# Moving half a unit of row norms, two head sums and a semaphore count inside a fused four-block network

## The reference

```
pQ, pK = elu(Q), elu(K)                       # 16 heads of 16
kv = einsum('bshe,bshd->bsed', K, V) * SCALE  # per row, over the heads
attn = w1 - lmb * w2                          # w = einsum(Q, kv), per row
attn = (1 - LAMBDA_INIT) * rms(attn, g2)      # head norm: over 16 numbers
attn = rms(attn, g3) + attn                   # row norm: over 256 numbers
h = gelu(attn @ W1.T);  out = h @ W2.T + attn
x = layernorm(x + out)
```

## Time and profile before

| | |
|---|---|
| median of 3 runs | 947.38 us (947.28 to 952.99) |
| profiled execution, its own time | 946.61 us |
| span of the profile | 945.0 us |
| mean granted clock of TensorE | 0.951 of full |
| busy PE / PEld / DVE / ACT / POOL | 831.6 / 688.2 / 616.9 / 482.5 / 254.4 us |

### The profile page before, as it was taken

One profiled execution on the slowest core, in us unless ns is written; L12 is line 12 of the kernel. 1 busy time (PEld: TensorE's weight loads), 2 busy tenths in 40 slices (PEclk: granted clock), 3 DMA queues, 4 the chain that ended last, 5 costly groups with the idle time before them and its releaser, 6 DMA issues. The chain is left out here.

```text
span 945.0 us, 23205 instructions
## 1 busy us (share of the span) xinstructions
PE 831.6 (88%) x8838; PEld 688.2 (73%) x8838; DVE 616.9 (65%) x1408; ACT 482.5 (51%) x999; POOL 254.4 (27%) x323
## 2 busy tenths in 40 slices
PE   5999999999799999998999889889888949999960
PEld 5777787877577777766677778776666738999960
DVE  2577777777557777777565435678666885666626
ACT  2544434434567777766964334554644232635425
POOL 1256655121112222223000000013232121656444
PEclk9999999999999999999999999999988858999995
DMA  8500000000000000002466344443222301657429
GB/s 320 168 18 17 22 17 17 17 17 2 1 1 1 1 1 1 1 1 68 130 184 187 94 116 114 119 125 132 90 91 73 106 20 40 200 136 213 120 40 345
DMA packets 76429, 79.56 MB, mean 84 GB/s; under 512 B 22592, under 2 KB 66496, under 8 KB 75968
## 3 DMA queue, kind: packets, MB, share of 16 engines
q1 hardware_dynamic: 71376, 72.36, 24.8%
q0 software_dynamic: 3968, 5.25, 3.2%
q10 hardware_dynamic: 1008, 0.91, 0.3%
HBM read 50.71 MB, written 27.79 MB: 83 GB/s over the span
## 5 line engine op out<-in xcount | busy, mean ns | idle before, releaser
L713 DVE TENSOR_TENSOR r_prob<-r_pS,const 128x512 f32<-128x512 f32 x128 | 79.4, 681 | 32.4 <-PE r_pS L540 32.4
L1087 DVE SCALAR_TENSOR_TENSOR f_gl<-att_res,small_first,f_gh 128x512 fp32r<-128x512 f32 x64 | 47.3, 747 | 37.3 <-ACT f_gh L1012 35.0
L941 PE MATMUL f_pY<-wpjT,f_gh 128*128 128x256 f32 x256 | 66.1, 292 | 0.3 <-DVE f_gl L1087 0.3
L942 PE MATMUL f_pY<-wpjT,f_gl 128*128 128x256 f32 x256 | 63.4, 281 | 0.0
L1347 PEld LDWEIGHTS q_bank<-q_xT,att_res 128*64 128x64 f32 x1024 | 55.6, 137 | 7.2 <-issue 4.2
L941 PEld LDWEIGHTS f_pY<-wpjT,f_gh 128*128 128x128 f32 x256 | 48.7, 190 | 15.9 <-issue 13.4
L2418 POOL DMA_INDIRECT sum_dram<-e_yo,y_id x24 | 43.1, 1796 | 63.5 <-ACT e_yo L2551 47.7
L1347 PE MATMUL q_bank<-q_xT,att_res 128*64 128x128 f32 x1024 | 59.2, 274 | 0.0
L1006 ACT ACTIVATE att_res<-f_pH 128x512 f32<-128x512 f32 x64 | 38.1, 595 | 40.1 <-PE f_pH L926 39.4
L2532 ACT ACTIVATE e_hh<-e_pH 128x320 fp32r<-128x320 f32 x64 | 26.2, 434 | 55.7 <-PE e_pH L2457 55.5
L837 POOL TENSOR_SCALAR t_ey<-t_es 128x8 f32<-128x8 f32 x4 | 0.8, 203 | 197.3 <-ACT t_sqrow L1908 197.3
(11 more groups left out here) (307 smaller groups left out, 2368.5 us busy)
## 6 DMA issues: line engine op xcount, KB each, us to landing
kv_dram<-att_res SPq DMA_DIRECT2D x32, 256.0 KB, 3.6
t_ring<-kv_dram SPq DMA_DIRECT2D x128, 64.0 KB, 2.4
wi<-L_ffn_wi SPq DMA_DIRECT2D x8, 1024.0 KB
wo<-L_ffn_wo SPq DMA_DIRECT2D x8, 1024.0 KB
x_res<-L_attn_x SPq DMA_DIRECT2D x8, 512.0 KB, 5.4
q_dram<-att_res SPq DMA_DIRECT2D x8, 512.0 KB, 3.0
t_q<-q_dram SPq DMA_DIRECT2D x64, 64.0 KB, 2.9
x_dram<-x_res SPq DMA_DIRECT2D x8, 512.0 KB, 3.0
```

What stands on the lines that cost most here:

```text
L713: dve.tensor_tensor(prob[t % 2][:, r, :, :], pS[r][:, :, :], dec[:, r, :, :], ALU.mult)\
L941: pe.matmul(out, gh[c % 4][:, cols], net.wpjT[:, c, :], start=(c == 0 and t % 2 == 0), stop=False, skip_group_check=True)
L942: mm = pe.matmul(out, gl[c % 4][:, cols], net.wpjT[:, c, :], start=False, stop=(c == NH - 1), skip_group_check=True)
L1087: dve.scalar_tensor_tensor(out=gl[c % 4][:, :], in0=g[c][:, :], scalar=net.lnw[:, c:c + 1], in1=gh[c % 4][:, :], op0=ALU.mult, op1=ALU.sub ...
```

## The change

Three edits. Each of the four clearing instructions raises `cleared` by itself, and PE waits for one bank ahead of `scores(0)`, for two ahead of `scores(1)`, and for all four ahead of the first `mix`. `last_row_norms` takes the pairs to do: pairs 0 and 2 stay where they were (DVE's `body(1)` and `body(3)`), pairs 4 and 6 go one body later: for unit 2 to the end of `body(2)`, ahead of `head_norm(3)`; for unit 3 to the end of `body(4)`, ahead of `choose(0, (0,))`. The sums of squares of the last two head quarters go from ahead of `body(0)` to between `rows(0)` and `norm(0)`. No instruction that computes is added or taken away.

```diff
@@ tensor
-        pe.wait_ge(cleared.sem, cleared.after(1))
         for n in range(ALL + 3):
+            if n < 2:
+                pe.wait_ge(cleared.sem, cleared.after(n + 1))
             if n < ALL:
                 scores(n)
             if n == 2:
-                pe.wait_ge(cleared.sem, cleared.after(2))
+                pe.wait_ge(cleared.sem, cleared.after(4))
@@ vector
-        def last_row_norms(u):
-
-            row_norm(u, 0)
-            for j in range(2, GROUPS, 2):
+        def last_row_norms(u, pairs):
+
+            for j in pairs:
+                if j == 0:
+                    row_norm(u, 0)
+                    continue
                 n = (GROUPS // 2 - 1) * (u - LAST + 1) + j // 2 - 1
                 dve.wait_ge(factors_ready.sem, factors_ready.after(n + 1))
                 pair = att[:, GROUPS * u + j:GROUPS * u + j + 2, :]
@@
         for banks in (pA, pO):
             for i in two:
-                ins = dve.memset(banks[i][:, :, :], 0.0)
-            ins.then_inc(cleared.sem, 1)
+                dve.memset(banks[i][:, :, :], 0.0).then_inc(cleared.sem, 1)
@@ body(b) of vector
             rows(b)
+            if b == 0:
+                sum_heads(LAST, 2)
+                sum_heads(LAST, 3)
@@
             if b == 1:
-                last_row_norms(LAST - 1)
+                last_row_norms(LAST - 1, (0, 2))
             if b == 2:
+                last_row_norms(LAST - 1, (4, 6))
                 head_norm(LAST)
             if b == 3:
-                last_row_norms(LAST)
+                last_row_norms(LAST, (0, 2))
+            if b == 4:
+                last_row_norms(LAST, (4, 6))
             if b == GB:
                 choose(0, (0,))
@@ ahead of body(0)
         scale_heads(LAST, 3)
-        sum_heads(LAST, 2)
-        sum_heads(LAST, 3)
```

## The result

| | before | changed |
|---|---|---|
| median of 12 runs | 949.73 us | 942.18 us |
| ratio, changed to before | | 0.9907 (0.9886 to 0.9927) |
| span of the profiled run | 945.0 us | 943.2 us |
| mean granted clock | 0.951 | 0.945 |

The account below looks back on a forecast made before the run. PE, the busiest engine, was taken as bound by waits for DVE's normed rows, each paid again by a slower clock. 0.5 + 2.4 + 5.3 = 8.2 us, giving 939.2 us from the median 947.38; range 934.5 to 944.5.

Parts of the forecast that it names:

- Edit 1: Score loop: a signal for each cleared bank lets `scores(0)` start sooner; gain 0.5 us, bounds 0 and 0.5.
- Edit 2: The two last head sums moved behind `rows(0)` shorten PE's wait at `turn_x(0, 0)`, clock stays; gain 2.4 us.
- Edit 3: Pairs 4 and 6 one body later: no PE wait at `turn_x(2, 0)` and `turn_x(4, 0)`; gain 5.3 us.
- The 0.88: Without the head sums ahead of it, the addition of `rows(0)` can start 0.88 us sooner.
- What is late next: POOL's `base(5)` falls among DVE's `head_norm(3)` steps and costs 2.2 us; PE waits 3.6 at b = 3.
- rival B: `base(5)` does not hold up `head_norm(3)`: total gain 11.8 or 13.0 us, time 934.4 to 935.6; chance 0.18.
- rival C: Gains stay local, BN statistics in `rows(2)` stand still beside `base`: 2 to 5 us gained, 942.4 to 945.4; chance 0.14.
- The 5.4 at `turn_x(2, 1)`: Unit 2's move: `turn_x(2, 0)` starts without a wait, so `turn_x(2, 1)` comes 5.4 us sooner.
- All of the 5.4 is gone at this point: At `turn_x(3, 1)`: 707.7 against 707.15 before, so unit 2's gain of 5.4 us is fully given back.
- Rival D: Slower: PE's clock falls in the expert stage at waits it now survives, 2.3 us a fall; 948.4; chance 0.04.

Follow-up runs that it names:

- small `base(5)`: Changed kernel with POOL's `base(5)` cut to 8 columns of one tile, leaving out nearly the whole residual of batch 5; ratio 0.9871 to the kernel before.
- edit 2 alone: Kernel before with only the two last head sums moved behind `rows(0)`; ratio 0.9973 to the kernel before.
- unit 2 alone: Kernel before with only unit 2's pairs 4 and 6 moved one body later, unit 3's left; ratio 0.9975 to the kernel before.
- Unit 3's move alone: Kernel before with only unit 3's pairs 4 and 6 moved one body later, unit 2's left; ratio 0.9928 to the kernel before.
- edit 1 alone: Kernel before with only a signal for each cleared bank; ratio 0.9995 to the kernel before.
- edit 3 alone: Kernel before with only pairs 4 and 6 of units 2 and 3 moved one body later; ratio 0.9936 to the kernel before.
- head norm first: Changed kernel with `head_norm(3)` ahead of unit 2's pairs 4 and 6 in DVE's `body(2)`; ratio 0.9859 to the kernel before.
- head norm split: Kernel of head norm first, with the first three steps of `head_norm(3)` put between `rows(2)` and `norm(2)`; ratio 0.9857 to the kernel before.

## Why the prediction was right

**The sum.** Forecast 8.2 us, measured 8.8 (6.9 to 10.8). The terms, against the profiles of the single edits:

- Edit 1, 0.5: the start is as forecast; at the end it is not measurable, and in both profiles of the changed kernel the loop came out longer than before, by 1.5 and 1.8.
- Edit 2, 2.4: 2.55 up to `turn_x(0, 1)`. The 0.88 is 0.87, the wait of 1.22 is 1.23, the clock stays. The sums needed 1.26 us and left 0.36, more room than the 0.1 to 0.2 that I gave.
- Edit 3, 5.3: 6.37. The mechanism is the one forecast at each `turn_x`. The size was off by 1.0 because the block at full clock is 3.89 and not 4.10 (twice 0.2; my row ended in a wait for ACT, 0.44 us on PEld at 707.15), the block at low clock 6.18 and not 6.4, the wait at b = 3 3.28 and not 3.6, and 0.1 of small change.

For lead and stage together the two last terms say 7.7, and 8.92 were measured; for the loop the first says 0.5 less, and it was 1.5 to 1.8 more. That the total of 8.8 lies so close to 8.2 is thus in part luck: two errors of opposite sign, and an interval that would have held 7 as well as 10. The parts in which the mechanism is shown are lead and stage.

**What is late next.** That `base(5)` would meet `head_norm(3)` and cost 2.2 us was the step on which the forecast rested against rival B. It cost 2.07, shown by the small `base(5)`. The rule of the Trainium skill (SBUF — State Buffer, "Who interferes with whom") agrees with these rows: 2.37 for 0.29 where both inputs lie in SBUF, 0.68 unchanged where one is in PSUM, and statistics unchanged too, which also takes the ground from rival C. The profile of edit 2 alone shows the order of arrival on which rival B hung: there DVE's 128x2048 multiplication starts at 690.77 and takes its usual 2.29 us, `base(5)` starts at 692.35 and takes 2.93 in place of 2.36, so the one that came second was the one to stand. Rival B's outcome did not come by itself; it came when the order was changed.

**Unit 2 against unit 3.** The 5.4 at `turn_x(2, 1)` was 5.78, and "All of the 5.4 is gone at this point" was short of the truth by 0.26 (0.12 with unit 2 alone). Unit 3's move alone is worth as much as both. What the reckoning did not have is that unit 2's move alone brings 2.05 at b = 4, as long as unit 3's pairs stand where they were; with both moved there is nothing left there to gain.

**Rival D in small.** The clock did fall at other places than before: in the loop of the changed kernel one fall accounts for all of the 1.5 us. In the profile before, a wait of 3.01 us ahead of the mix at 624.83 left the clock at 1.00; in the changed kernel the same wait, 2.90, was followed by 0.59. Both stand 94.77 us behind the first clear, and from there to `turn(0)` are 17.63 and 19.16 us. Timeline and window of the kernel before, then of the changed one:

```profile
624.83 1.07 PE L1708 MATMUL t_pO<-t_ring,t_scT 128*16 128x128 f32 x32 [3.01 <-DVE t_scT L2020]
```

```profile
625.00:628.00 3.00, 3.00 (x68) 2.62 (x64) 2.87 (x7) 2.13 (x7) 0.00 (x0) 1.00 0.47 124
```

```profile
630.60 1.07 PE L1708 MATMUL t_pO<-t_ring,t_scT 128*16 128x128 f32 x32 [2.90 <-DVE t_scT L2021]
```

```profile
631.00:634.00 3.00, 3.00 (x38) 2.79 (x28) 1.99 (x6) 1.88 (x7) 0.00 (x0) 0.59 0.52 139
```

The other profiles have a wait of 2.89 to 3.05 us at the same place, 93.7 to 95.1 us behind the first clear. Where the clock stays (before, edit 1 alone, edit 3 alone, each unit alone, small `base(5)`) there are 17.60 to 17.66 us from the mix to `turn(0)`; where it falls (edit 2 alone, both profiles of the changed kernel, head norm first, head norm split) 18.96 to 20.44. So this one fall makes the long loops, 112.9 to 115.4 against 111.3 to 112.4. The wait doesn't tell them apart: 2.89 stands in both groups, the others that fell had 2.90 to 2.96, and the others that stayed 2.95 to 3.05. The five that fell all have edit 2, which changes nothing in the loop, and four of them edit 1, which moves PE's start by 0.5 us; but edit 1 alone and the small `base(5)`, which has both, did not fall. With one or two profiles of each I can't say whether this is more than chance. It stays open.

## What to carry to other kernels

When a strictly ordered engine is freed earlier at one batch, follow the gain to the next meeting of two queues before counting it: here 5.5 of 5.8 us that unit 2 had gained vanished because an engine that had been late until then now arrived in the middle of a neighbour's work. Work that one engine must finish before another may start (pairs 4 and 6 ahead of `base(5)`) is also a handle: placed behind the sensitive steps, it keeps the other engine away from them. And where the clock of an untouched part moves by more than the edit is worth, compare blocks between fixed instructions and leave the spans alone.

## What the runs showed of the hardware that was not expected

The granted clock does not follow from the length of a wait alone: after 1.21 us at the same place it was 1.00 in one kernel and 0.50 in another, and after 2.89 to 3.05 us in the score loop it stayed in six profiles and fell in five, while all waits of 1.23 at b = 0 (six profiles) kept it, and all of 2.09 and 2.10 there (five profiles), the one of 2.28 and all of 3.19 to 3.28 in the second part lost it. For a forecast this means a chance and a price (1.3 to 2.8 us a fall), not a threshold. Between profiles of one program the first clear came at 535.83 and 533.14, a spread of 2.7 us ahead of any changed instruction; over all kernels it lay between 530.06 and 537.69.
